# Rows of x fetched straight to where the sorted pairs will lie, and the edge-feature copies issued by ScalarE

## What is computed

```python
edge_sum = segment_sum(edge_attr, src, num_segments=50000)
h = elu(concat([x, edge_sum], 1) @ W0 + b0)      # 256 -> 128
h = elu(h @ W2 + b2)
out = layernorm(x + h @ W3 + b3)
```

## Time and profile before

| | |
|---|---|
| time, median of 3 runs | 602.74 us (598.56 to 602.87) |
| the profiled execution | 601.51 us, its span 599.7 us |
| PE busy | 534.1 us (89%) |
| DVE busy | 492.7 us (82%) |
| ACT busy | 434.4 us (72%) |
| POOL busy | 371.2 us (62%) |
| chain that ended last | PE 57%, DVE 17%, issue 12%, ACT 6%, SPq 3% |
| DMA traffic | 97.06 MB, mean 162 GB/s |

### The profile page before, as it was taken

One profiled execution on the slowest core, in us unless ns is written; L12 is line 12 of the kernel. 1 busy time (PEld: TensorE's weight loads), 2 busy tenths in 40 slices (PEclk: granted clock), 3 DMA queues, 4 the chain that ended last, 5 costly groups with the idle time before them and its releaser, 6 DMA issues.

```text
span 599.7 us, 11136 instructions
## 1 busy us (share of the span) xinstructions
PE 534.1 (89%) x2890; PEld 363.3 (61%) x2890; DVE 492.7 (82%) x1391; ACT 434.4 (72%) x1632; POOL 371.2 (62%) x310
## 2 busy tenths in 40 slices
PE   3899999779999999999899988788999999999980
PEld 1355555456566666677666655456676767777650
DVE  5988899788999989798888876667898888988961
ACT  2477775758888888786777774657788887888841
POOL 7766658466672778877887777785444333344306
PEclk9999999989999999999999999989999999999986
DMA  4567878677785777766666653344433444433101
GB/s 140 161 195 231 235 224 258 196 222 238 224 269 175 236 222 201 196 173 181 182 174 184 172 154 115 104 121 119 117 107 119 132 124 121 122 91 94 54 37 52
DMA packets 87766, 97.06 MB, mean 162 GB/s; under 512 B 26403, under 2 KB 56595, under 8 KB 87703
## 3 DMA queue, kind: packets, MB, share of 16 engines
q1 hardware_dynamic: 58807, 71.06, 37.8%
q0 software_dynamic: 28896, 25.29, 17.7%
HBM read 58.10 MB, written 45.04 MB: 172 GB/s over the span
## 4 chain that ended last, share of the span: by engine, by line
PE 57%; DVE 17%; issue 12%; ACT 6%; SPq 3%; another core or an unknown queue 1%; DMA 1%; POOL 1%; POOLq 0%; ACTq 0%; DVEq 0%
PE z_ps L568 13%; PE z_ps L569 13%; PE l_ps L524 11%; PE l_ps L556 11%; DVE e L862 4%; PE sum_ps L500 4%; ACT sq L638 3%; DVE h L865 3%; PE l_ps L535 3%; DVE o_sb L896 1%; PE turn_ps L549 1%; DMA x_sb<-x_items_dram 1%; SPq L323 1%; DVE net L759 1%
## 5 line engine op out<-in xcount | busy, mean ns | idle before, releaser
L638 ACT ACTIVATE sq<-z_ps 128x128 f32<-128x128 f32 (+1 forms) x493 | 129.8, 279 | 118.7 <-PE z_ps L569 68.1
L568 PE MATMUL z_ps<-center,xT 128*128 128x128 f32 (+1 forms) x986 | 194.5, 279 | 11.1 <-DVE h L865 9.6
L418 POOL DMA_INDIRECT out_dram<-pair_edge,target_i x100 | 120.5, 1205 | 122.4 <-issue 106.5
L569 PE MATMUL z_ps<-w3c,h 128*128 128x128 f32 (+1 forms) x986 | 191.1, 276 | 0.0
L568 PEld LDWEIGHTS z_ps<-center,xT 128*128 128x128 f32 (+1 forms) x986 | 153.5, 192 | 60.6 <-DVE h L865 30.6
L865 DVE SCALAR_TENSOR_TENSOR h<-l_ps,neg_bias,e 128x512 f32<-128x512 f32 (+1 forms) x214 | 159.1, 744 | 7.6
L397 POOL DMA_INDIRECT x_early<-in_x_dram,src_i x100 | 123.8, 1238 | 58.5 <-DMA pairs_dram<-x_early 28.6
L629 ACT ACTIVATE e<-l_ps,bias 128x512 f32<-128x512 f32 (+1 forms) x214 | 143.4, 670 | 13.4 <-PE l_ps L524 5.3
L407 POOL DMA_INDIRECT pair_edge<-pairs_dram,edge_i x100 | 124.0, 1240 | 42.6 <-issue 30.2
L569 PEld LDWEIGHTS z_ps<-w3c,h 128*128 128x128 f32 (+1 forms) x986 | 150.0, 192 | 0.0
L524 PE MATMUL l_ps<-xT,w0x 128*128 128x512 f32 (+1 forms) x248 | 131.7, 613 | 17.3 <-issue 12.5
(11 more groups left out here) (131 smaller groups left out, 372.7 us busy)
## 6 DMA issues: line engine op xcount, KB each, us to landing
x_sb<-x_items_dram SPq DMA_DIRECT2D x98, 256.0 KB
out_dram<-o_sb SPq DMA_DIRECT2D x98, 256.0 KB
pairs_dram<-x_early SPq DMA_DIRECT2D x25, 250.0 KB
keyB<-key_rows_dram SPq DMA_DIRECT2D x25, 250.0 KB
pairs_dram<-in_edge_attr_dram SPq DMA_DIRECT2D x24, 256.0 KB
x_early<-in_x_dram,src_i POOLq DMA_INDIRECT x100
pair_edge<-pairs_dram,edge_i POOLq DMA_INDIRECT x100
out_dram<-pair_edge,target_i POOLq DMA_INDIRECT x100
```

Source lines behind the costliest of these rows:

```text
L418: nc.gpsimd.indirect_dma_start(out=out[:, :], out_offset=bass.IndirectOffsetOnAxis(ap=target_i[0:EP, c:c + 1], axis=0), in_=pair_edge[0:EP ...
L568: T.matmul(z, xT[:, c % SLOTS, j * q:(j + 1) * q], center[:], start=True, stop=False)
L569: mm = T.matmul(z, h2[:, c % 2, j * q:(j + 1) * q], w3c[:], start=False, stop=True)
L638: t = A.activation(sq[0:q, j, :], z_ps[c % 2][0:q, j * P:(j + 1) * P], ACT.Square, scale=float(P) ** -0.5, accum_out=ssq[0:q, c % 2, j:j + 1])
```

## The change

`fetch_x` writes straight into `pair_edge[..., 0:P]`, the columns into which the gather will later write the sorted pairs; the tile `x_early`, its four slots and POOL's wait for them are gone, and there is one `x_fetched` semaphore for each g and one `x_paired` in all. `pair_x(g)` copies from `pair_edge` and moves from step 2 + 3g//2 to step 2 + 7g//6, so g = 24 stands in step 30. `pair_attr(g)` moves from SP to ScalarE, at the head of its step 2 + g. Rows, bytes and the number of DMAs stay the same.

```diff
-    PAIR_X = {2 + 3 * g // 2: g for g in range(NE)}
+    PAIR_X = {2 + 7 * g // 6: g for g in range(NE)}
...
-        x_early = sb("x_early", [P, SLOTS, J, P])
...
-        x_fetched = [sem(f"x_fetched{k}") for k in range(SLOTS)]
-        x_paired = [sem(f"x_paired{k}") for k in range(SLOTS)]
+        x_fetched = [sem(f"x_fetched{g}") for g in range(NE)]
+        x_paired = sem("x_paired")
...
             def pair_x(g):
-                k = g % SLOTS
-                sp.wait_ge(x_fetched[k], 16 * J * (g // SLOTS + 1))
+                sp.wait_ge(x_fetched[g], 16 * J)
                 sp.dma_start(pairs.rearrange("(p c) f -> p c f", p=EP)[:, J * g:J * g + J, 0:P],
-                             x_early[0:EP, k, :, :]).then_inc(x_paired[k], 16)
-
-            def pair_attr(g):
-                last = min(E, ROWS * (g + 1))
-                sp.dma_start(pairs[ROWS * g:last, P:2 * P], attr[ROWS * g:last, :]).then_inc(attr_paired, 16)
+                             pair_edge[0:EP, J * g:J * g + J, 0:P]).then_inc(x_paired, 16)
...
-                if c in PAIR_ATTR:
-                    pair_attr(PAIR_ATTR[c])
...
             def fetch_x(g):
-                k = g % SLOTS
-                at_least(pool, x_paired[k], 16 * (g // SLOTS))
-                for j in range(J):
+
+                for c in range(J * g, J * g + J):
                     nc.gpsimd.indirect_dma_start(
-                        out=x_early[0:EP, k, j, :], out_offset=None, in_=x[:, :],
-                        in_offset=bass.IndirectOffsetOnAxis(ap=src_i[0:EP, J * g + j:J * g + j + 1], axis=0),
-                    ).then_inc(x_fetched[k], 16)
+                        out=pair_edge[0:EP, c, 0:P], out_offset=None, in_=x[:, :],
+                        in_offset=bass.IndirectOffsetOnAxis(ap=src_i[0:EP, c:c + 1], axis=0),
+                    ).then_inc(x_fetched[g], 16)
...
-            for k in range(SLOTS):
-                pool.wait_ge(x_paired[k], 16 * len(range(k, NE, SLOTS)))
+            pool.wait_ge(x_paired, 16 * NE)
...
+            def pair_attr(g):
+                last = min(E, ROWS * (g + 1))
+                act.dma_start(pairs[ROWS * g:last, P:2 * P], attr[ROWS * g:last, :]).then_inc(attr_paired, 16)
...
             for c in range(STEPS_END):
+                if c in PAIR_ATTR:
+                    pair_attr(PAIR_ATTR[c])
                 parts = []
```

## The result

The changed kernel took 624.19 us (median of 5, 622.55 to 628.09) where the kernel before, beside it on the same chip, took 602.87 us (median of 5). The ratio is 1.037, its 95% interval 1.033 to 1.042. It is slower; the forecast was 598.5 us. In this document medians are of all executions, while ratios and their intervals leave out those in which the chip was in a slower state. The profiled execution of after took 628.09 us with a span of 626.3 us, 26.6 us more than the span of before.

The account below looks back on a forecast made before the run. TensorE, busy 89% of the span, was taken as the bound, so gains must come from stretches where it waits. The sum was 601.5 - 6.5 + 2 + 1 = 598.0 us, stated as 598.5, range 591 to 608.

Parts of the forecast that it names:

- POOL's denser fetches: Before 155 us, POOL's fetches without slot waits would change DMA traffic but no item pace: 0, at most +2 us.
- the slow stretch: Edge stage, 352 to 412 us, 6.0 us an item: taken as proportional to POOL's scatter backlog, 4.4 us less.
- Fetches ending at 155 us: On POOL, the 100 fetches would run back to back and end at 155 us instead of 183.8.
- Gather from 168, scatters from 324: On POOL, the gather would start from about 168 us and the scatters at about 324, 28 us earlier.
- -6.5 us in the edge stage: Edge stage: 2.3 us less beside the gather and 4.4 us less from a smaller scatter backlog, taken as -6.5 us.
- SP's waits, +2: SP's queue up to step 30: waits for fetches before pair copies, about 3 us at the last, +2 us taken.
- The hope for another 4 us from SP's long load issue: SP's queue at 143.89 us: a 4.78 us load issue might shrink by 4 us without feature copies; not in the sum.
- ScalarE's issues, +1: ScalarE, steps 2 to 26: 25 feature-copy issues of 0.50 us, covered in the sort; +1 us for steps 21 to 26.
- ScalarE pays: Rival, chance 0.12: each issue at the head of ScalarE's 25 steps is paid in full, 12.6 us, giving 610 us.
- Slower, 0.14, and 591 to 608: Whole kernel: chance 0.14 of being slower by over 1%, above 608.8 us, and a forecast range of 591 to 608 us.

Follow-up runs that it names:

- slots8_b: The kernel before with eight slots of `x_early` instead of four: 618.9 us, ratio 1.026 on a slower chip; 567.14 us, ratio 1.001 on the faster chip.
- after_b: The changed kernel unchanged, run again beside the kernel before on a slower chip: 625.13 us, ratio 1.036.
- fetch_paced2: The changed kernel with fetch g waiting for pair copy g-4, on the faster chip: 572.8 us, ratio 1.011.
- attr_act_only: The kernel before with only the feature copies moved from SP to ScalarE, on a slower chip: 610.28 us, ratio 1.011.
- attr_sp: The changed kernel with the feature copies back on SP, on a slower chip: 622.15 us, ratio 1.026.
- interleaved_b: The kernel before with six gathers ahead, then scatter(g) and gather(g+6) in turn, on a slower chip: 578.08 us, ratio 0.957.

## Why the prediction was wrong

- **The step that failed** is the sentence on "POOL's denser fetches": "no item pace followed it ..., so 0, with +2 as the upper end". It asked what the fetches do to the DMA engines' share, found that 0.64 and 0.79 both gave 4.0 us, and priced the removal of 28.6 us of POOL's waits at nothing. The DMA share fell in after (0.68 against 0.77), so fuller DMA engines are indeed not what slowed the sort. But the waits had another effect: they broke up POOL's stream. Without them the run to 160 us lost 8 items. `slots8_b`, where nothing but the slots differs, prices this term at 2.6%, some 16 us, where the prediction had 0 to +2; after's trace shows it as the late answers.
- **The evidence was in the earlier trace rows and was read too narrowly.** I saw that the slow stretch coincided with a POOL that didn't pause and made of it a cost of the *edge stage's backlog*, worth something when it shrinks. I didn't ask whether the change makes another such stretch.
- **Fetches ending at 155 us**: right. **Gather from 168, scatters from 324**: wrong (195.3 and 351.8). The fetch was ready; the pair copy's step wasn't. A due time that is a step number moves with the pace of the steps.
- **-6.5 us in the edge stage**: in the profile of after the changed kernel did win 2 items there, 8 us, but not by an earlier gather. The first edge item finishes at 284.3 us instead of 252.0, so with scatters from 351.8 us (352 - 285)/13.9 = 4.8 groups wait instead of 7.1. With the smaller backlog POOL's first longer pause begins at 399.9 us instead of 410.7, and the slow stretch ends earlier with it. But the gain did not repeat. In `after_b` POOL's first longer pause begins even earlier, at 388.6 us, and the late answers end there, yet they begin at 267 us, and from 236 to 412 us 35 items finish, as many as in before:

```profile
236.00:412.00 176.00, 23.84 (x35) 0.99 0.57 157
```

So the end of the slow stretch follows POOL's backlog, but the stretch isn't the backlog's alone, and the -6.5 us isn't borne out.
- **SP's waits, +2**: right in size by luck. SP waited once, 2.0 us, for a fetch, in the trace of after, and that was before 40 us. In the steps from 21 to 30, where the prediction put the wait, there was none: the slow steps gave the fetches time, so that its mechanism was not tried at the 4.0 us pace. On the faster chip, where the steps are quicker, `fetch_paced2` had 2.9 us of such waits between 100 and 130 us. The waits of SP's queue in after (us in total, times, longest; the earlier trace rows):

```profile
SPq L329 <- DVE o_sb L892: 280.2, 65, 12.3
...
SPq L338 <- DMA pair_edge<-in_x_dram,src_i: 2.0, 1, 2.0
```

- **The hope for another 4 us from SP's long load issue**, which the prediction kept out of its sum: rightly left out. With the feature copies gone from SP the longest issue of a load took 4.78 us in after and 4.93 us in `attr_act_only`, against 4.78 us in before.
- **ScalarE's issues, +1**: too small. Alone they cost 1.1% (0.6 to 1.7%), some 3 to 10 us, and ScalarE's waits before the squares in the sort grew (26.9 us, against 11.2 us in the earlier trace rows) where the prediction had them 0.5 us a step shorter. The rival "ScalarE pays" had the sign and named a sorting stretch slower than 4.75 us as its mark; the mark came, but `attr_sp` and `slots8_b` give most of it to POOL.
- **Set against the sum**: some 16 us for POOL's waits in place of 0, some 6 us for ScalarE's issues in place of 1, and no sure gain in the edge stage in place of -6.5 make about 27 us, an estimate, where the miss was 624.2 - 598.5 = 25.7 us.
- **Slower, 0.14, and 591 to 608**: all rivals took their prices from one engine being held up by a wait or by its own work. None let an engine off the path slow the hand-over between two others, though before's own stretch of 6.0 us an item was an example of it.

What stays open: why TensorE's answers come late, what starts it, and why only on some chips. Shown is that on a slower chip they are tied to POOL's DMAs: more slots alone bring them (`slots8_b`), they end with the first pause there, and another order of the same DMAs avoids nearly all of them in the edge stage (`interleaved_b`). Each of these rests on one kernel on one chip, and by which path POOL's DMAs act isn't shown. Open too is why they need more than the stream, and what the new pair steps cost on a slower chip.

## What to carry to other kernels

A wait of an off-path engine that costs it nothing may protect the others: before removing one, look for a stretch in the same trace where that engine already runs without waits, and read the pace there. If a slow stretch can't be explained by any busy engine, find its cause first and treat every place to which the change spreads its conditions as a possible second one. Of the kernels measured, the one with scatters and gathers in turn and everything else as before is the one to keep: 0.957 where late answers occur and 1.000 where they don't.

## What the runs showed of the hardware

- The same kernel took 567, 578 and 603 to 606 us on different chips, and the change cost 3.6% on a slower one, 1.6% on the middle one. The chips differ in whether TensorE's answers come late while POOL streams DMAs: `slots8` has none on the faster chip, `slots8_b` 31 on a slower one. A result measured on one chip holds for that chip, until it is repeated on another.
- A late answer cost ScalarE 0.4 to 4.3 us of waiting before the squares, 2.4 us on average (74.6 us in 31 waits in after). The granted clock of these stretches was lower (0.95 in the sort of after and 0.83 from 104 to 132 us, against 1.00 and 0.94 in before). The late answers came first: five stand between 44 and 76 us, at 1.00.
- TensorE's answers to VectorE were late in the same steps as those to ScalarE (2.08 us for a product of the sort, 4.06 us for layer 3).
- An indirect DMA took POOL 1.21 us and 0.30 us between two, whether it wrote to `x_early` or to `pair_edge`; the destination made no difference.
- A DMA issue on ScalarE took 0.50 us, 0.40 us of it exposed before the next activation, and 25 of them cost 1.1% on a slower chip, where two activations of the size of one block's squares (0.28 us) in the same places cost nothing that could be measured (0.999).
